# A second feed-forward norm: a scale folded into the weights' split, and two small steps given to GpSimd

## What is computed

```python
def ternary_quant(w):
    scale = 1.0 / jnp.clip(jnp.mean(jnp.abs(w)), 1e-05)
    wq = jnp.clip(jnp.round(w * scale), -1.0, 1.0) / scale
    return w + jax.lax.stop_gradient(wq - w)
h = layer_norm(x, ln1_g, ln1_b)
h = jnp.einsum('bsd,hd->bsh', h, ternary_quant(w1)) + b1
h = jax.nn.gelu(h, approximate=False)
h = layer_norm(h, ln2_g, ln2_b)             # over the 1024 hidden channels
out = jnp.einsum('bsh,dh->bsd', h, ternary_quant(w2)) + b2
...
x = _layernorm(x + attention(x))
x = _layernorm(x + ffn(x))
```

## Time and profile before

| | |
|---|---|
| median of 3 runs | 578.0 us (577.88 to 579.27) |
| profiled execution, first to last instruction | 576.0 us |
| TensorE, matmul busy | 538.8 us, 94% |
| TensorE, weight load busy | 490.9 us, 85% |
| VectorE | 504.5 us, 88% |
| ScalarE | 483.0 us, 84% |
| GpSimd | 396.8 us, 69% |
| mean granted clock of TensorE | 0.987 |
| HBM | 29.0 MB read, 16.8 MB written |

### The profile page before, as it was taken

How to read it: one execution, slowest core, us unless ns; L and a number is a source line. 1 busy time by engine, 2 the same in 40 slices (tenths; PEclk the granted TensorE clock), 3 DMA queues, 4 the chain that set the end, 5 groups by cost and what they waited for, 6 DMA issues and landing times.

```text
span 576.0 us, 10831 instructions
## 1 busy us (share of the span) xinstructions
PE 538.8 (94%) x3522; PEld 490.9 (85%) x3522; DVE 504.5 (88%) x1280; ACT 483.0 (84%) x949; POOL 396.8 (69%) x385
## 2 busy tenths in 40 slices
PE   2989999999999999989899999999999999999990
PEld 2879999989999999978778988888998888889890
DVE  3779898997889899867677999999999999999986
ACT  3472879799988978875989999999999999999983
POOL 0466678969597987578439768766767866675672
PEclk9989999999999999999999999999999999999996
DMA  5632014050524112033110022221022222110102
GB/s 175 264 118 75 2 42 180 1 220 2 194 99 162 60 47 102 10 153 133 73 38 2 37 74 75 74 73 53 23 74 74 75 75 75 39 36 38 38 38 109
DMA packets 11399, 46.52 MB, mean 81 GB/s; under 512 B 1360, under 2 KB 1744, under 8 KB 9168
## 3 DMA queue, kind: packets, MB, share of 16 engines
q1 hardware_dynamic: 11344, 45.83, 21.7%
HBM read 29.02 MB, written 16.81 MB: 80 GB/s over the span
## 4 chain that ended last, share of the span: by engine, by line
PE 72%; DVE 12%; ACT 9%; DMA 3%; issue 2%; POOL 1%; SPq 0%; ACTq 0%; DVEq 0%; POOLq 0%
PE ring L1795 20%; PE qps_sps_aps_then_y L1819 20%; PE qps_sps_aps_then_y L1668 7%; PE ring L1610 6%; PE qps_sps_aps_then_y L1592 5%; PE qps_sps_aps_then_y L1685 5%; PE ring L1737 2%; DVE z L1123 2%; DMA xc<-in_x_chan_dram 2%; PE ring L1712 2%; PE ring L1700 1%; PE ring L1750 1%; DVE qsum L1017 1%; PE qps_sps_aps_then_y L1643 1%; DMA x_scratch<-z 1%
## 5 line engine op out<-in xcount | busy, mean ns | idle before, releaser
L1819 PE MATMUL qps_sps_aps_then_y<-ff_w_over_xc_lo,ff_a_lo_over_qw 128*128 128x258 f32 x512 | 126.3, 283 | 0.0
L1819 PE MATMUL qps_sps_aps_then_y<-ff_w_over_xc_lo,ff_a_hi_over_xc_lo 128*128 128x258 f32 x512 | 126.3, 283 | 0.0
L1795 PE MATMUL ring<-ff_ht_hi_over_qw,t 128*128 128x512 f32 x256 | 105.6, 413 | 0.9 <-DVE ff_ht_lo_over_xc_hi L1195 0.5
L1795 PE MATMUL ring<-ff_ht_lo_over_xc_hi,t 128*128 128x512 f32 x256 | 101.1, 395 | 0.0
L1819 PEld LDWEIGHTS qps_sps_aps_then_y<-ff_w_over_xc_lo,ff_a_hi_over_xc_lo 128*128 128x128 f32 x512 | 96.9, 189 | 3.5
L1819 PEld LDWEIGHTS qps_sps_aps_then_y<-ff_w_over_xc_lo,ff_a_lo_over_qw 128*128 128x128 f32 x512 | 96.6, 189 | 3.4
L1203 DVE SCALAR_TENSOR_TENSOR ff_a_lo_over_qw<-ring,ff_rho,ff_a_hi_over_xc_lo 128x512 fp32r<-128x512 f32 x128 | 91.5, 741 | 6.1 <-ACT ff_a_hi_over_xc_lo L772 5.0
L754 ACT ACTIVATE ring<-ring,bias 128x512 f32<-128x512 f32 x128 | 84.0, 677 | 11.4 <-PE ring L1795 10.2
L512 POOL TENSOR_TENSOR ff_accp_over_xt_lo<-ff_accp_over_xt_lo,ff_sq_over_ek_et_hi 128x512 f32<-128x512 f32 x64 | 84.3, 1318 | 5.0 <-POOL ff_accp_over_xt_lo L512 0.4
L770 ACT ACTIVATE ff_sq_over_ek_et_hi<-ring 128x512 f32<-128x512 f32 x128 | 79.0, 617 | 0.5
L772 ACT CAST ff_a_hi_over_xc_lo<-ring 128x512 fp32r<-128x512 f32 x128 | 77.8, 608 | 0.0
(11 more groups left out here) (173 smaller groups left out, 1625.4 us busy)
## 6 DMA issues: line engine op xcount, KB each, us to landing
x_scratch<-z SPq DMA_DIRECT2D x16, 514.0 KB, 3.0
ff_x_over_w_raw_xc<-x_scratch SPq DMA_DIRECT2D x16, 514.0 KB, 4.6
xt<-in_x_tok_dram SPq DMA_DIRECT2D x8, 1024.0 KB, 4.9
out_dram<-ff_z_over_et_lo SPq DMA_DIRECT2D x15, 512.0 KB, 3.4
xc<-in_x_chan_dram SPq DMA_DIRECT2D x7, 1024.0 KB, 6.7
w_raw<-in_w_dram SPq DMA_DIRECT2D x2, 1024.0 KB, 5.9
xc<-in_x_chan_dram SPq DMA_DIRECT2D x2, 512.0 KB, 5.9
out_dram<-ff_z_over_et_lo SPq DMA_DIRECT2D x2, 256.0 KB, 2.7
```

What stands on the lines that cost most here:

```text
L1795: mm = nc.tensor.matmul(ff_bank(k, m), t1[:, c, m * P:(m + 1) * P], h[:, k % 2, c], start=(c == 0 and j == 0), stop=(c == CH - 1 and j == 1))
L1819: last = nc.tensor.matmul(ff_yps[:, t, 0:C + 2], a[:, m % DEPTH, t * P:(t + 1) * P], ff_w2[:, m], start=(m == 0 and j == 0), stop=(m == FC ...
```

## The change

Three things are changed, all in small operations.

1. **The second step goes into the norm's weights.** `ff_split_gain` now multiplies `ln2_g` by `wstep[:, 1:2]`, once into the rounded `ff_g_hi` and once into the full `ff_g_all`, ahead of the split; it has nine operations instead of eight. Since it needs the second step, it moves from the end of round `b = 0` to the end of round `b = 6`. The row `ff_u_row` is multiplied by the step too. So `ff_yc` has the step in it, `ff_gain` goes away, and the residual multiplies by `ff_rsH`. What is left of `ff_residual_gain` are its waits (`ff_residual_free`), and `ff_hidden_rstd` waits on GpSimd until the residual before has read `ff_rsH`.
2. **The square of the mean goes to GpSimd**, as `ff_mean_square`, between the first and the second of its additions of squares; it waits for the mean.
3. **The output's epsilon goes to GpSimd**, in `ff_out_rstd`, ahead of the power; it waits for the aggregates.

```diff
@@ GpSimd
                 pool.wait_ge(ff_r_eps, k + 1)
+                wait_for(pool, ff_z_ok, TB * k)
                 nc.gpsimd.tensor_tensor(ff_rsH[:], ff_var[:], nhalf[:, 0:TB], ALU.pow).then_inc(ff_r_rstd, 1)
 
+            def ff_mean_square(k):
+                if not 0 <= k < NK:
+                    return
+                pool.wait_ge(ff_r_mean, k + 1)
+                wait_for(pool, ff_r_var, k)
+                nc.gpsimd.tensor_tensor(ff_msq[:], ff_nmu[:], ff_nmu[:], ALU.mult).then_inc(ff_r_sq, 1)
+
             def ff_out_rstd(k):
                 if not 0 <= k < NK:
                     return
+                pool.wait_ge(ff_z_var, TB * (k + 1))
+                nc.gpsimd.tensor_tensor(ff_veZ[:], ff_mvZ[:, :, 1], eps[:, 0:TB], ALU.add).then_inc(ff_z_eps, 1)
                 pool.wait_ge(ff_z_eps, k + 1)
...
                 ff_keep_residual(k - 1, 1)
                 ff_square_sum(k - 1, 1)
+                ff_mean_square(k - 2)
                 ff_square_sum(k - 1, 2)
                 ff_hidden_rstd(k - 2)
@@ VectorE, folded_rows
-                nc.vector.tensor_copy(ff_u_row[:], qps[:, 0:C]).then_inc(f_out, 1)
+                nc.vector.tensor_scalar(ff_u_row[:], qps[:, 0:C], wstep[:, 1:2], None, ALU.mult).then_inc(f_out, 1)
@@ VectorE, ff_split_gain
-                nc.vector.tensor_copy(ff_g_hi[:], g).then_inc(ff_g_step, 1)
+                dve.wait_ge(f_step, 2)
+                nc.vector.tensor_scalar(ff_g_hi[:], g, wstep[:, 1:2], None, ALU.mult).then_inc(ff_g_step, 1)
+                nc.vector.tensor_scalar(ff_g_all[:], g, wstep[:, 1:2], None, ALU.mult).then_inc(ff_g_step, 1)
...
-                nc.vector.tensor_tensor(ff_g_all[:], g, ff_flat[:], ALU.add).then_inc(ff_g_step, 1)
+                nc.vector.tensor_tensor(ff_g_all[:], ff_g_all[:], ff_flat[:], ALU.add).then_inc(ff_g_step, 1)
@@ VectorE, ff_hidden_stats
-                nc.vector.tensor_tensor(ff_msq[:], ff_nmu[:], ff_nmu[:], ALU.mult).then_inc(ff_r_sq, 1)
                 dve.wait_ge(ff_r_sum, k + 1)
                 dve.wait_ge(ff_r_sq, k + 1)
@@ VectorE, ff_residual_gain, now ff_residual_free
                 dve.wait_ge(ff_r_rstd, k + 1)
-                nc.vector.tensor_scalar(ff_gain[:], ff_rsH[:], wstep[:, 1:2], None, ALU.mult).then_inc(ff_r_gain, 1)
-                dve.wait_ge(ff_r_gain, k + 1)
@@ VectorE, ff_residual
-                        out=ff_z[:, k % 2, t], in0=ff_yc[:, t], scalar=ff_gain[:, t:t + 1], in1=ff_x1c[:, k % 2, t],
+                        out=ff_z[:, k % 2, t], in0=ff_yc[:, t], scalar=ff_rsH[:, t:t + 1], in1=ff_x1c[:, k % 2, t],
@@ VectorE, ff_out_variance
-                dve.wait_ge(ff_z_var, TB * (k + 1))
-                nc.vector.tensor_scalar(ff_veZ[:], ff_mvZ[:, :, 1], EPS, None, ALU.add).then_inc(ff_z_eps, 1)
@@ VectorE, attention's loop
-                if b == 0:
+                if b == 6:
                     ff_split_gain()
```

More of the change, by code:

```diff
@@ L169, in both_halves @@
         ff_rsH = sb("ff_rsH", [P, TB])
-        ff_gain = sb("ff_gain", [P, TB])
         l_ve, l_rs, l_shift = sb("l_ve", [P, TB]), sb("l_rs", [P, TB]), sb("l_shift", [P, TB])
@@ L254, in both_halves @@
         ff_sum_p, ff_sum_d = sem("ff_sum_p"), sem("ff_sum_d")
-        ff_r_tr, ff_r_sum, ff_r_mean, ff_r_sq, ff_r_var, ff_r_eps, ff_r_rstd, ff_r_gain = (
-            sem(s) for s in ("ff_r_tr", "ff_r_sum", "ff_r_mean", "ff_r_sq", "ff_r_var", "ff_r_eps", "ff_r_rstd", "ff_r_gain"))
+        ff_r_tr, ff_r_sum, ff_r_mean, ff_r_sq, ff_r_var, ff_r_eps, ff_r_rstd = (
+            sem(s) for s in ("ff_r_tr", "ff_r_sum", "ff_r_mean", "ff_r_sq", "ff_r_var", "ff_r_eps", "ff_r_rstd"))
         ff_yc_ok, ff_z_ok, ff_z_stat, ff_z_var, ff_z_eps, ff_z_rstd, ff_z_nmr, ff_o_ok = (
@@ L564, in _ @@
             ff_square_sum(1, 1)
+            ff_mean_square(0)
             ff_square_sum(1, 2)
@@ L574, in _ @@
             ff_square_sum(2, 1)
+            ff_mean_square(1)
             ff_square_sum(2, 2)
@@ L1250, in ff_hidden_stats, with ff_residual_free @@
                 nc.vector.tensor_scalar(ff_var[:], ff_var[:], 0.0, EPS, ALU.max, ALU.add).then_inc(ff_r_eps, 1)
-            def ff_residual_gain(k):
+            def ff_residual_free(k):
                 if not 0 <= k < NK:
@@ L1471, in _ @@
                 ff_out_variance(k - 2)
-                ff_residual_gain(k - 1)
+                ff_residual_free(k - 1)
                 ff_act_low(k, 5)
@@ L1494, in _ @@
             ff_out_variance(NK - 3)
-            ff_residual_gain(NK - 2)
+            ff_residual_free(NK - 2)
             ff_act_low(NK - 1, 5)
@@ L1510, in _ @@
             ff_out_variance(NK - 2)
-            ff_residual_gain(NK - 1)
+            ff_residual_free(NK - 1)
             ff_residual(NK - 1, (0, 1))
```

12 lines of the change are left out of this document (6 added, 6 removed).

## The result

| | before | after |
|---|---|---|
| median us | 578.63 (577.88 to 579.34, 4 runs) | 572.16 (570.05 to 572.64, 4 runs) |
| ratio, 95% interval | | 0.9879 [0.9861, 0.9897] |
| profiled execution, span us | 576.0 | 570.7 |
| TensorE, matmul busy | 538.8 (94%) | 534.3 (94%) |
| VectorE busy | 504.5 (88%) | 479.5 (84%) |

The change makes the kernel 1.2% faster. The forecast was 572.8. VectorE lost 25 us of busy time over the span; the kernel became 5.3 us shorter by the two profiles and 6.5 by the medians. (All runs were made beside runs of the kernel before on the same chip; its medians lay between 578.2 and 578.9.)

A forecast was written before the change was run, and what follows sets the result against it. VectorE was taken to pace the steady feed-forward rounds at 16.93 us, TensorE's floor being 16.48. 576.0 - 5.2 (rounds) - 0.4 (tail) + 0.4 (split) = 570.8, with 2.0 from span to median 572.8 us; range 571.4 to 577.0.

The forecast's parts named there:

- VectorE paces the steady rounds, TensorE 0.45 under it: Feed-forward rounds: VectorE, in order, takes 16.93 us; TensorE could do 16.48 and waits 0.45.
- The saving of 0.45 a round, 5.2 in all: Feed-forward rounds fall from 16.93 to TensorE's 16.48; summed over the rounds above that floor, 5.2 us.
- VectorE at 16.18, 0.3 to spare: Steady feed-forward rounds: removed operations save VectorE 0.75 us, 16.93 to 16.18, which is 0.3 under TensorE's 16.48.
- rival 4: Feed-forward rounds: one more VectorE pair meets GpSimd's additions, rounds of 17.22, 581.4 us, slower; chance 0.07.
- The price of each removal: VectorE's steady round, by distance between starts: ff_veZ 0.43 us, ff_gain 0.25, ff_msq 0.07.
- GpSimd's additions are free: Steady rounds: GpSimd's added square and epsilon, 0.21 us each, cost zero; 0.3 us a round if cover were gone.
- The split in round 6: End of attention round 6: nine VectorE operations take 1.6 us, make TensorE's transposes 0.45 late; carried as +0.4 us.
- The tail, -0.4: After the last matmul, VectorE's chain loses 0.32 for ff_veZ and ff_gain and 0.07 for ff_msq: -0.4 us.
- forecast tie: Tail: GpSimd's addition and power end at 568.0, shift wanted at 568.1; if missed, 0.1 to 0.2 us lost.
- TensorE pacing already: Rival 1, feed-forward rounds: they stay 16.93 because TensorE already paces, leaving 578.0 us; chance 0.13.
- ScalarE taking over half way: Rival 2, feed-forward rounds: ScalarE, own round about 16.2 us, leaves half the gain, 575.4 us; chance 0.10.
- The split meets no GpSimd operation: Against rival 3: in round 6 the split meets GpSimd, 5.25 us instead of 1.6, giving 576.4; chance 0.06.

The follow-up runs named there:

- the six added operations: Six extra bn_stats of 0.33 us per feed-forward round on VectorE, added to the kernel after: 584.19 us, ratio 1.0097.
- the fold: Kernel after with square and epsilon back on VectorE, keeping the second step in the norm's weights and split in round 6: 572.81 us, ratio 0.9898.
- the square alone: Kernel before with only the square of the mean moved to GpSimd: 577.26 us, ratio 0.9971.
- the epsilon alone: Kernel before with only the output norm's epsilon moved to GpSimd: 573.5 us, ratio 0.9909.
- the split in the gap: Kernel after with the split gain behind k_maximum(NB - 1, 0), where VectorE idles: 570.29 us, ratio 0.9857; also tried in three other versions.

## Why the prediction was right, and where it was not

**VectorE paces the steady rounds, TensorE 0.45 under it: shown.** Two operations added to the kernel before came through in full (0.65 for 0.66); the same two added to the kernel after did not. The pieces of eight matmuls are equal, as forecast.

**The saving of 0.45 a round, 5.2 in all: measured 6.46.** The mechanism was right, and the term mis-sized by the floor. The twelve rounds from 331.27 to 533.82 took 202.55 us; the same ones now take 529.39 - 332.75 = 196.64. Of the 5.9 between them 4.8 are the forecast's sum for these rounds, and 12 x 0.09 = 1.1 are the lower floor. The prediction took 16.48 from a round of before as something that no edit here touches ("no TensorE instruction changes"), and 16 bytes less of SBUF touched it.

**VectorE at 16.18, 0.3 to spare: the step that failed, without effect on the time.** It was reckoned as 16.93 less the removed 0.75, with all else at its old duration. The pair of 1.91 is not a constant. The prediction named this in rival 4 ("I rather expect one meeting fewer") and left it out of the sum. The spare time was 1.2 us by the waits and 1.5 by the six added operations. Had TensorE's floor been lower, the sum would have been wrong by up to 1 us a round. It also carried into the expectations of the parts: they used the price of each operation and not what its removal moves.

**The price of each removal.** ff_veZ and ff_gain by distance between starts: in their own terms right, but the two are not independent. ff_veZ cost 0.43 because it ended with GpSimd's addition; when it goes, ff_gain waits in its place (0.64). ff_msq was worth its 0.14 and not 0.07.

**GpSimd's additions are free: right.** 0.21 and 0.20 us, as the earlier trace rows had it. The square stands behind the first addition, in idle time, and 1.62 us of waiting for ff_var follow it. With the fold there they are also worth nothing.

**The split in round 6: the operations right, what followed not.** They take from 239.18 to 240.73, 1.55 us (1.6 forecast), meet no long operation of GpSimd, and make the transposes late:

```profile
239.18 0.20 DVE L1173 TENSOR_SCALAR ff_g_hi<-vecs,wstep 128x8 fp32r<-128x8 f32 x1
...
240.62 0.17 DVE L1187 TENSOR_SCALAR ff_sig<-ff_flat 128x8 f32<-128x8 f32 x1
240.73 0.48 DVE L1135 SCALAR_TENSOR_TENSOR z<-z,rsA,xt 128x256 f32<-128x256 f32 x1
```

By the timelines the transposes begin at 245.88 instead of 245.35, 0.53 late. The forecast's 0.4 took their start, 245.46, from the chain, where the piece before covers their first 0.11 us; VectorE's result was thus wanted 0.06 us after its end and not 0.15.

But the projection's result, read at 249.86 before, was read at 252.01, 2.15 late, with the clock's fall in between. By the first feed-forward round 1.52 were left. The prediction carried a lateness through the chain as a constant and did not ask what the clock would do behind an idle time of TensorE. The move costs about 2 us (four pairs of medians differ by 1.9 to 2.3, the fourth being 573.84 - 571.97 = 1.9), not 0.4.

What the clock does there goes with the idle time, though not always. In the six profiles with the split in round 6 TensorE waits 0.42 to 0.55 us ahead of the transposes, and in five of them the clock falls to between 0.50 and 0.60 in a stretch of 2 us. In the eight without it (before, before with two added operations, the square alone, the epsilon alone, and the four with the split in the gap) there is no idle time there and the clock is 1.00 throughout. The sixth is the version with the 16-byte tile, late like the others:

```profile
245.58 0.44 PE L1645 MATMUL qps_sps_aps_then_y<-ident,r_f 128*128 128x128 f32 x2 [0.54 <-DVE r_f L1094]
```

```profile
248.00:252.00 4.00, 4.00 (x23) 3.35 (x22) 1.75 (x6) 2.29 (x5) 3.33 (x6) 1.00 0.35 144
```

```profile
250.09 0.87 DVE L1109 SCALAR_TENSOR_TENSOR r_f<-u_row,nmean,qps_sps_aps_then_y 128x256 f32<-128x256 f32 x2 [1.93 <-PE qps_sps_aps_then_y L1653]
```

This one separates the two costs. From the start of the transposes to the reading of the projection it takes 250.09 - 245.58 = 4.51 us, as the eight profiles without the idle time do (4.49 to 4.53); the five in which the clock fell take 6.11 to 6.15 (after: 252.01 - 245.88 = 6.13). The fall costs 1.6 us there, and the lateness of the transposes 0.5 besides. In each of the six kernels with the split in round 6 the run with the highest mean clock is also the shortest (after: 0.993 with 570.05, against 0.986 to 0.989 with 571.85 to 572.64), as if the fall came in most executions and not in all. Only the mean clock of these runs is known, and in the kernel before it does not sort the times (0.992 with 579.2, 0.988 with 578.2), so that link stays open.

**The tail, -0.4: right, -0.36.** The forecast tie was missed, though:

```profile
561.60 0.35 POOL L493 TENSOR_TENSOR ff_veZ<-ff_mvZ,eps 128x4 f32<-128x4 f32 x1 [1.62 <-DVE ff_mvZ L1294]
562.03 1.12 POOL L496 TENSOR_TENSOR ff_rsZ<-ff_veZ,nhalf 128x4 f32<-128x4 f32 x1
```

```profile
563.19 0.16 DVE L1316 SCALAR_TENSOR_TENSOR ff_nmr<-ff_mvZ,ff_rsZ 128x4 f32<-128x4 f32 x1 [0.23 <-POOL ff_rsZ L496]
```

Beside the residual pair GpSimd's addition took 0.35 and the power 1.12, against 0.20 and 1.02 in the rounds, and the shift waited 0.23.

**The sum** was right within 0.7 us partly by luck, because two misses cancel: the floor gave 1.1 more, the clock and what hangs on it took 1.1 more (1.52 against 0.4). Profile to profile it is -5.3 against -5.2; the rest is the distance from span to median, 1.5 instead of 2.0.

**The rivals.** TensorE pacing already, and ScalarE taking over half way, fell with the rounds of 16.39. The split meets no GpSimd operation. The two engines have one meeting fewer, not one more. The rule of the Trainium skill, GPSIMD Engine Reference, section "Key points", that GpSimd and VectorE contend for SBUF, agrees with the pair of 1.91 and 0.87, whose operations read two tiles in SBUF. Read as a warning against more small operations on GpSimd it did not decide here: the version with them and the one without differ by 0.35 us.

## What to carry to other kernels

An operation on the engine that paces is worth its own time plus what its going does to the meetings of the operations behind it: lay the two engines' orders over each other after the edit before pricing it, and try the smallest part of an edit alone, since beyond the next engine's floor the rest brings nothing. Small work that is moved belongs in a stretch where its engine waits for TensorE anyway, not ahead of a result for which TensorE will wait; half a microsecond there cost some four times its length. Compare the floor of the next engine in kernels with the same tiles allocated, or allow it 0.5%.

## What the runs showed of the hardware

- **SBUF placement changes the rate of matmuls.** An unused tile of 16 or 32 bytes a partition makes eight matmuls of 512 columns take 1.86 to 1.88 us instead of 1.83 to 1.85, 0.09 us in a round of 16.4, and 1.7 us in the median of the runs. Which tile's address does it is open.
- **The granted clock fell behind a short idle time.** After the change TensorE stood 0.54 us without a matmul, then came transposes and 16 matmuls of two columns (shown as 1.93 us, clock 1.00), and in the next 4 us the clock was 0.57. It fell in five profiles of six with the idle time, and in none of eight without; each fall cost 1.6 us. Idle time alone did not do it: with the split in the gap TensorE waited 0.50 us up to 252.01, ahead of other matmuls, and the clock stayed at 1.00.
- **A small VectorE operation can last until GpSimd's long one ends.** ff_veZ took 0.51 to 0.52 us with 0.2 of work; when it is taken away, ff_gain takes 0.64 in its place. Not every small operation is held: the three aggregations of 439.43 take 0.28 us in all beside the same additions. Beside GpSimd's power on four elements, which lasts 1.02 us, VectorE's residual pair is not held up: 0.87 us.
